# Last attention of a four-layer kernel: one sum of probabilities is issued three TensorE steps later

## The reference, cut to what matters

```python
for e in range(4):
    xn = _layernorm(x[:, e*n:(e+1)*n, :], norm_w, norm_b)
    m = d // 2 ** e
    xm = xn[..., :m]          # q, k, v from the first m columns
...
attn = jax.nn.softmax(jnp.einsum('bhqd,bhkd->bhqk', q, k) * scale, axis=-1)
attn_out = jnp.einsum('bhqk,bhkd->bhqd', attn, v)
...
out = jnp.einsum('bnm,om->bno', attn_out[:, sl, :m], o_w[:m, :m]) + o_b[:m]   # then + x, and a layernorm
```

## Time and profile before

| | |
|---|---|
| time, median of 3 runs | 2575.21 us (2572.23 to 2576.28) |
| the profiled execution: its time | 2573.41 us |
| the profiled execution: its span, first to last instruction | 2571.6 us |
| mean granted TensorE clock | 0.954 |
| busy share of the span: PE / PEld / DVE / ACT / POOL | 85% / 53% / 55% / 39% / 35% |
| POOL in the last quarter, tenths in slices of 64.3 us | 7 to 8 |
| last layer's POOL adds (L1689 + L1691), busy | 277.3 us + 149.6 us |
| all PE matmuls of the sums (L1881, `added` alone) | 468, from 1910.2 us to 2535.0 us |

### The profile page before, as it was taken

One profiled execution on the slowest core, in us unless ns is written; L12 is line 12 of the kernel. 1 busy time (PEld: TensorE's weight loads), 2 busy tenths in 40 slices (PEclk: granted clock), 3 DMA queues, 4 the chain that ended last, 5 costly groups with the idle time before them and its releaser, 6 DMA issues.

```text
span 2571.6 us, 42553 instructions
## 1 busy us (share of the span) xinstructions
PE 2186.2 (85%) x17140; PEld 1373.2 (53%) x17140; DVE 1412.4 (55%) x2526; ACT 994.9 (39%) x1450; POOL 898.9 (35%) x573
## 2 busy tenths in 40 slices
PE   2899999999999999678878689999688888888885
PEld 1445555555555455466666447766455555555553
DVE  2445555545555555356565445545467777677672
ACT  1133333333333333255434333334244544554443
POOL 4122222222222220012222122111447777777784
PEclk7799999999999999899999999999789999999997
DMA  6555555555555553256786741101654364436411
GB/s 133 104 105 127 108 108 110 121 108 108 108 108 118 111 107 62 107 200 228 273 284 224 271 158 66 33 33 50 176 143 116 97 174 132 133 96 166 117 43 50
DMA packets 226386, 328.86 MB, mean 128 GB/s; under 512 B 14368, under 2 KB 163984, under 8 KB 225936
## 3 DMA queue, kind: packets, MB, share of 16 engines
q1 hardware_dynamic: 219200, 321.56, 47.8%
q10 hardware_dynamic: 6992, 4.60, 0.6%
HBM read 197.53 MB, written 127.93 MB: 127 GB/s over the span
## 4 chain that ended last, share of the span: by engine, by line
PE 26%; DVE 11%; POOL 7%; DMA 6%; issue 2%; ACT 2%; SPq 2%; ACTq 0%; POOLq 0%; DVEq 0%
DVE l1f_rowmax L1812 4%; PE l1a_slot L1412 4%; POOL l1f_added L1689 4%; PE l1a_slot L1403 2%; POOL l1f_added L1691 2%; DMA l0f_f<-in_dram 2%; PE l1a_slot L1454 2%; SPq L879 2%; PE l1f_slot L1943 2%; PE l1f_os L1867 2%; DMA l0f_x<-x 2%; PE l0f_slot L1120 2%; PE l1f_slot L1934 2%; PE l0f_slot L1113 1%; PE l1a_slot L1424 1%
## 5 line engine op out<-in xcount | busy, mean ns | idle before, releaser
L534 ACT ACTIVATE l0a_probs<-l0a_slot 128x1024 f32<-128x1024 f32 (+1 forms) x256 | 248.4, 971 | 336.0 <-PE l0a_slot L694 188.7
L591 DVE TENSOR_REDUCE l0a_rowmax<-l0a_slot 128x4 f32<-128x1024 f32 (+1 forms) x256 | 293.3, 1156 | 130.0 <-PE l0a_slot L704 127.0
L1761 ACT ACTIVATE l1f_probs<-l1f_slot 128x1024 f32<-128x1024 f32 x240 | 243.9, 1022 | 272.3 <-PE l1f_slot L1943 264.7
L1689 POOL TENSOR_TENSOR l1f_added<-l1f_probs 128x1024 f32<-128x1024 f32 x117 | 277.3, 2370 | 153.8 <-ACT l1f_probs L1761 153.8
L1812 DVE TENSOR_REDUCE l1f_rowmax<-l1f_slot 128x1 f32<-128x1024 f32 x240 | 287.1, 1216 | 65.2 <-PE l1f_slot L1934 64.7
L494 POOL TENSOR_TENSOR l0a_turned<-l0a_turned 128x512 f32<-128x512 f32 x32 | 40.7, 1273 | 557.0 <-DVE l0a_turned L577 557.0
L1943 PE MATMUL l1f_slot<-l1f_Qs,l1f_Ks 128*128 128x256 f32 x960 | 171.7, 303 | 38.4 <-DVE l1f_lo L1802 14.8
L1934 PE MATMUL l1f_slot<-l1f_Ks,l1f_Qs 96*128 96x512 f32 x480 | 176.7, 453 | 25.3 <-DVE l1f_rowmax L1812 18.6
L1943 PEld LDWEIGHTS l1f_slot<-l1f_Qs,l1f_Ks 128*128 128x128 f32 x960 | 144.3, 195 | 96.1 <-DVE l1f_rowmax L1812 33.3
L694 PE MATMUL l0a_slot<-l0a_mask,l0a_ident 128*128 128x512 bf16 (+1 forms) x512 | 150.3, 376 | 25.6 <-issue 23.3
L636 PE MATMUL l0a_O<-l0a_probs,l0a_V 128*32 128x128 f32 x3840 | 156.5, 279 | 10.6 <-issue 10.6
(11 more groups left out here) (196 smaller groups left out, 3931.4 us busy)
## 6 DMA issues: line engine op xcount, KB each, us to landing
expert_outputs<-l0f_wide SPq DMA_DIRECT2D x64, 512.0 KB, 3.3
l0f_wide<-expert_outputs SPq DMA_DIRECT2D x32, 1024.0 KB, 11.3
l0a_Qs<-qk_rows SPq DMA_DIRECT2D x96, 256.0 KB, 7.7
l0a_Ks<-qk_rows SPq DMA_DIRECT2D x96, 256.0 KB, 14.8
l1f_Ks<-kq_rows SPq DMA_DIRECT2D x48, 512.0 KB, 8.5
l0f_f<-in_dram SPq DMA_DIRECT2D x10, 2048.0 KB, 15.6
qk_rows<-l0a_hi SPq DMA_DIRECT2D x32, 512.0 KB, 2.8
qk_rows<-l0a_lo SPq DMA_DIRECT2D x32, 512.0 KB, 4.2
```

Source lines behind the costliest of these rows:

```text
L534: exp_ready.by(act.activation(probs[:, t % 2, HG * g:HG * g + HG, 0:reach, :], s[:, :, 0:reach, :], ACT.Exp, scale=SCALE))
L591: max_ready.by(dve.reduce_max(rowmax[:, t, :, 2 * g:2 * g + 2], s[:, :, :, first:2 * P], AX))
L1689: halved.by(pool.tensor_tensor(added[:, u, :], probs[:, 0, u, :], probs[:, 1, u, :], ALU.add))
L1761: exp_done.by(act.activation(probs[:, half, u - FIRST[b], :], s[:, :], ACT.Exp, scale=SCALE))
```

## The change

For the third batch alone, the sum leaves the end of stage seven and is put into stage eight in front of its second natural scores (nat 9). So mT 0, nat 8 and tr 27 now stand in front of it on TensorE, and add 12 on GpSimd in the list of steps. No operation is added, removed or altered.

```diff
@@ -1509,12 +1509,16 @@
         if half:
             row = [step for at in row for step in ([at, (0, "add", FIRST[i] + at[2] - tr[0][2])] if at in tr else [at])]
             row[4:4] = [(placing[0], "place", placing[1])]
+            if i == NB - 1:
+                at = row.index(nat[1])
+                row[at:at] = [(summing[0], "sum", summing[2])]
             for h in range(2):
                 at = row.index(nat[1 + h]) + 1
                 row[at:at] = [(*summing[:2], 2 * summing[2] + h)]
         else:
             summing = (0, "norms", i - 1) if i else (-1, "norms", NB - 1)
-            row += [(summing[0], "sum", summing[2]), (o, "mT", part // 2)]
+            row += [(summing[0], "sum", summing[2])] if i < NB - 1 else []
+            row += [(o, "mT", part // 2)]
             placing = o, part // 2
         steps += row
```

## The result

The changed kernel takes 2555.31 us (median of 4 runs, 2551.93 to 2558.44) against 2575.08 us before. The ratio is 0.9913 with a 95% interval of 0.9897 to 0.9928: it is faster by 0.87%, with bounds of 0.72 and 1.03%. A second set of runs gave 0.9912 (0.9897 to 0.9926). One execution of all that are reported here, of after_long, took 7675 us against 2563 to 2579 us for its others; the ratios leave it out.

A forecast was written before the change was run, and what follows sets the result against it. PE's wait for POOL at sum 2 was taken to lie on the binding chain; 9.1 + 4.8 + 0.8 = 14.7 us off 2573.41 us gave 2558.7 us, plus 1.8 us for the median 2560.5 us, range 2554 to 2569 us.

The forecast's parts named there:

- The wait and what is put into it: At sum 2, PE work placed inside the wait for POOL gains 1.3 us in each of seven sequences, 9.1 us.
- the upper bound: Behind sum 2, PE's gain per sequence: tr 28 starts 1.48 us sooner.
- the lower one: Behind sum 2, VectorE's gain per sequence: nat 9's row maximum ends 1.21 us sooner.
- The clock: Behind sum 2, in four of seven sequences, the falls of PE's clock vanish: 4 x 1.2 = 4.8 us.
- two such falls elsewhere that happen to go: Upper bound of the clock gain: 4.8 us plus two falls away from sum 2, 7.2 us in all.
- The last sequence: At its sum 2, which waits 7.37 us, only tr 27 passes in front: 0.8 us gained.
- over 6 us: Sign of being right: in the last sequence PE's wait for POOL before sum 2 is still over 6 us.
- the falls stay as many: Rival: short waits elsewhere meet as many clock falls; only 9.9 us won, 2565.3 us; chance 0.22.
- Given back later: Rival: PE reaches sum 2 after POOL, so the gain is lost; 2575 us, or 2570 us without falls; chance 0.14.
- Slower by VectorE and POOL hindering each other: Rival: in stage eight POOL's sooner adds and doubling overlap more of VectorE's chain and lengthen it; 2580 us; chance 0.05.

The follow-up runs named there:

- after_long: The changed kernel with tr 28 computed four times in place of once, behind the sum: 2569.5 us, ratio 0.9978.
- filler: The kernel before, order untouched, with tr 26 computed four times in front of sum 2's wait: 2573.1 us, ratio 0.9981.
- past_mT: The kernel before with only mT put in front of sum 2; nat 8 and tr 27 stay behind it: 2575.6 us, ratio 0.9992.
- before_tr27: The changed kernel with sum 2 one step sooner, only mT and nat 8 in front of it: 2561.3 us, ratio 0.9942.
- after_again: The changed kernel unaltered, timed and profiled once more: 2555.9 us, ratio 0.9912.
- nat9_longer: The changed kernel with sum 2 one step later, behind nat 9, and tr 28 computed twice: 2555.5 us, ratio 0.9918.
- behind_nat9: The changed kernel with sum 2 one step later, behind nat 9: 2553.8 us, ratio 0.9911; run again 2552.3 us, 0.9912.
- sum0_early: The changed kernel with sum 0 also moved, in front of the second output projection (out 1): 2555.7 us, ratio 0.9924.
- both: The changed kernel with sum 0 in front of out 1 and sum 2 behind nat 9: 2551.5 us, 0.9909; run again 2551.2 us, 0.9899.

## Why the prediction was right and where it was too small

**The wait and what is put into it: right.** The forecast was 1.3 us a body for seven bodies, 9.1 us. Measured at full clock it is 83.15 (from filler) - 81.72 = 1.43 us, the upper bound (1.48 us, PE's) nearly, not the lower one (1.21 us, VectorE's). The lighter seventh stretch went from 2533.74 - 2459.36 = 74.38 us to 2518.34 - 2445.36 = 72.98 us, with nearly the same mean clock (0.94 and 0.95), though the falls lie at other places: 1.40 us. Together 6 x 1.43 + 1.40 = 10.0 us. past_mT, before_tr27 and the changed kernel give 0, 0.95 and 1.43 us for 0.03, 0.57 and 1.05 us of PE work in front of the sum: the gain follows the work that is done inside the wait, a little more than one for one. The surplus of about 0.4 us I can only argue: nat 8's maximum is then also taken inside the wait, so that tr 28 no longer waits for it, and VectorE's chain starts from nat 9 alone.

**The clock: the step that was mis-sized.** The prediction said "I take it that the falls at this place vanish: 4 x 1.2 = 4.8 us", and bounded the rest by "two such falls elsewhere that happen to go". The first half is right: filler, which does that alone, gained 4.9 us by its ratio and has no fall behind sum 2, and 1.2 us was a fair price for these four. The bound was wrong. Eight of nine falls went, four of them in the stages three and four, and those cost more, 1.4 to 1.7 us each (84.7 - 83.15 = 1.55 us in the first body before), so the term is 20.5 - 10.0 = 10.5 us in place of 4.8. The five falls of the stages three and four were taken as given because their wait is not touched. The runs show that the wait alone does not decide whether it meets a fall. The reading that fits them best is that the place of the wait from body to body decides, and so the length of the body. Four profiles with full-clock bodies of 81.6 to 82.4 us (changed, after_again, before_tr27, nat9_longer) have 1, 0, 0 and 0 falls in 24 bodies. Bodies that are longer (82.9 to 83.2 us: after_long, filler) or shorter (80.9 to 81.4 us: behind_nat9 twice, sum0_early) have 3 to 5 in six. after_long and nat9_longer move a kernel out of that length and another one into it by added work alone, and the falls come and go with it. For after_long its time and its mean clock bear that out; for nat9_longer it rests on one profile. Length at full clock is not the whole of it: both has 80.3 us and had six falls in one execution and two in another. The change happened to move the body from 83.15 to 81.7 us. That this took the falls of stage three away was luck: one step further (behind_nat9) three and four are back.

The Trainium skill ("TensorE: Matmul & The Clock Gate", section on what is actually happening) says that the span over which activity is judged runs free of the kernel. I had cited it as a reason why falls might remain, and did not follow it to the point that a loop of constant length can come to nearly the same place in that span in each pass, and so escape a fall, or be caught, again and again. The traces fit that: six falls 81.9 us apart in one execution of both, and none in six bodies of 81.7 to 81.9 us in after_again. No run shows the span itself. Why exactly 81.6 to 82.4 us is clear of the falls, and why both has six falls in one execution and two in another, is not settled here.

**The last sequence.** Sum 2 waits 5.70 us there, not over 6 us as I wrote: tr 27 fills 0.7 us of the 7.37 us, and a fall of the clock somewhat ahead of it made PE 1 us later at this place, which cost nothing, as POOL was later still. From sum 2 to the sum of the last batch:

```profile
2518.34 1.93 PE L1885 MATMUL l1f_os<-l1f_added,opening_ones 128*32 128x256 f32 x16 [5.70 <-POOL l1f_added L1695]
...
2526.18 3.63 PE L1885 MATMUL l1f_os<-l1f_probs,opening_ones 128*32 128x256 f32 x48
```

That is 7.84 us. The same sum before:

```profile
2542.88 3.63 PE L1881 MATMUL l1f_os<-l1f_probs,opening_ones 128*32 128x256 f32 x48
```

With sum 2 at 2533.74 us it is 2542.88 - 2533.74 = 9.14 us, so 1.3 us were won where I took 0.8. It was given back in the output projection behind it, which ran wholly at the low clock this time: behind the last sum 2 the span has 38.2 us more, 37.8 us before.

**The rivals.** That the falls stay as many is what past_mT shows for an order without the gain, and not this kernel. Given back later: the sum still starts within 0.1 us of POOL's last add, and nothing downstream ate the gain. Slower by VectorE and POOL hindering each other: the 240 row maxima have a mean of 1216 ns on both pages, and three in a row under adds take 3.47 us in both the earlier trace rows.

## What to carry to other kernels

When an engine waits at the head of its queue for a slow neighbour, look at what stands right behind the wait and does not need its result: put in front, it came off the loop here at least one for one, up to the length of the wait (0.95 and 1.43 us for 0.57 and 1.05 us of work), and it is worth counting in the other engines' work that it lets start. Price TensorE's clock by whole loop bodies, not by the one wait: a body that becomes some tenths of a us longer or shorter can gain or lose a fall in many of its passes, which here was half of the whole gain of the layer. So time orders that differ by little, and compare bodies at the full clock, before one is called better.

## What the runs showed of the hardware

A wait of 1.07 us on an otherwise busy PE was followed by a fall of the clock in some bodies and not in others of the same kernel, and one fall cost 1.2 to 1.7 us of a body of 80 to 85 us. Adding 0.48 us of matmuls to a body took the falls in six bodies from 3 or 4 to 0, and the seven bodies became 0.9 to 2.7 us shorter in the profile; adding 1.44 us to another brought them from 1 or 0 to 5. In one execution six falls came 81.9 us apart, one in each body behind the same waits.
